# Score and value segments of an 8-head attention placed next to each other on TensorE, with the values in rotating PSUM banks and the sums of exponentials in the score banks

## The chip, the core and the metric

The kernel runs on one core of one Trainium2 chip. The metric is the device time of one execution in microseconds, here the median of three runs: 2110.87 us (2109.59 to 2112.22).

## The reference, cut

Four attention blocks follow each other on a tensor of 64 images, 256 channels and 14 by 14 pixels (196 tokens). The first (L0) has a depthwise convolution, keys and values resized to 7 by 7, and a small network behind it. The second (L1) is a linear attention. The third (L2), which the change touches, is a full attention with 8 heads of 32 channels. The fourth (L3) is a full attention with one head.

```python
hid = _group_norm(xr, norm_w, norm_b)
qkv = jnp.einsum('oc,bcl->bol', qkv_w, hid) + qkv_b[None, :, None]
...
weight = jnp.einsum('bhct,bhcs->bhts', q * scale, k * scale)
weight = jax.nn.softmax(weight.astype(jnp.float32), axis=-1).astype(weight.dtype)
a = jnp.einsum('bhts,bhcs->bhct', weight, v)
...
h = jnp.einsum('oc,bcl->bol', proj_w, h) + proj_b[None, :, None]
...
return (x + h) / RESCALE
```

## The kernel before

**Pairs and turns.** Two images make a pair, and 32 pairs run through a software pipeline. A turn of the loop starts one pair and ends one; in between some seven pairs are at work, each at another stage. What an engine does in a turn, and in which order, stands in five dictionaries (`SP_AT`, `PE_AT`, `ACT_AT`, `DVE_AT`, `POOL_AT`): each step has a number, its remainder by 128 is its place in the turn and its quotient is the number of turns by which its pair lags. The numbers are places and no times: an engine runs its list in order and waits, by semaphores, for what a step needs. The function `step` of each engine goes over the 128 places.

**Names of the steps.** L0: `q0`, `k0`, `v0`, `s0` (scores), `t0` (transposes), `o0`, `pw`, `mlp`. L1: `kv0` to `kv3`, `keys` (keys scaled by ScalarE), `q1`, `ctx0` and `ctx1` (keys by values), `out`. L2: `hq`, `hk`, `hv` (queries, keys, values), `sc0` to `sc3`, `tn`, `av0` to `av3`, `proj`. L3: `q3`, `v3`, `s3`, `t3`, `o3`. Ahead of L1, L2 and L3 stands a group norm: `gn1` to `gn3` on TensorE is a product of 8 columns with a matrix of ones by group.

**L2 in detail.** The 16 head-images of a pair are worked on in four groups g of four heads (HG = 4).
- `sc{g}` (from L1240 on): TensorE takes the four heads side by side, each in 32 rows of the array, once for each half of the tokens: eight products of 98 by 196, each head into a PSUM bank of its own (`ps_s`, four banks). In f32 each product is two instructions, so the trace shows 16.
- `max{g}_{m}` (L958): VectorE takes the maxima of two banks.
- `sc{g}_{j}` of ScalarE (L822): two exponentials for each head, with their sums through the accumulator output into `den2` in SBUF. Each is followed by an accumulator read in the trace.
- `rden{g}_{m}` (L1063): VectorE's reciprocals of four sums (two heads by two halves).
- `less{g}_{j}` (L830): ScalarE scales the exponentials.
- `tn{g}_{j}` (L1222): TensorE transposes them back into the same bank; ScalarE copies them to `pt2` (L836).
- `av{g}` (L1226): TensorE multiplies by the values, four heads side by side, each in 32 columns of the array: again 16 instructions, into bank 0 of `ps_s`. ScalarE and VectorE read the result as a high and a low part (L843, L1069).

A matmul that uses only 32 rows or only 32 columns of the array is called tiled below, one that uses it whole is called whole.

**Banks.** PSUM has eight banks. Four are `ps_s`. The other four, `a`, `b`, `c`, `e`, are plain: the steps listed for each in `BANK_USES` use it one after the other in the order of TensorE's list. A step may fill a bank when all readers of the step before it in that bank have read. The helper `product` and most matmuls go through `mm` (L1167), so the tile, not the line, tells the step.

The score banks' uses before are:

```python
bank_s = [Bank(f"bank_s{j}", ps_s[:, j], [
    use for g in range(GROUPS) for use in (
        (f"sc{g}_{j}", PE_AT[f"sc{g}"], 2), (f"tn{g}_{j}", PE_AT[f"tn{g}_{j}"], 1),
        *([(f"av{g}", PE_AT[f"av{g}"], 1)] if j == 0 else []))]) for j in range(HG)]
```

**TensorE's order in a turn, before** (places 0 to 127): tn2_1, gn2, tn2_2, k0, tn2_3, tn2_0, o3_0, pw1, **sc3**, s0_0, q3_1, v3_1, **av2**, v3_2, s0_1, mlp0, mlp1, q3_0, v3_0, v3_3, tn3_1, tn3_0, tn3_2, hk0, tn3_3, hq0, gn1, v0, t0_0, t0_1, **sc0**, s3_0, o0_1, o0_0, hv1, **av3**, hv0, s3_1, tn0_1, hq1, tn0_0, tn0_2, proj1, tn0_3, hk1, proj0, **sc1**, kv0, kv1, **av0**, kv2, t3_0, kv3, gn3, q1_0, tn1_1, q1_1, q0_1, tn1_3, tn1_0, tn1_2, ctx0, ctx1, **sc2**, q0_0, t3_1, out0, out1, **av1**, o3_1, pw0.

## Time and profile before

| | |
|---|---|
| median of three runs | 2110.87 us |
| the profiled execution | 2112.12 us |
| its span | 2109.7 us |
| granted TensorE clock, mean over the span | 0.98 |
| chain that ended last, share of the span | TensorE 88%, ScalarE 4%, VectorE 1% |
| HBM read and written | 30.85 and 12.85 MB |

The profiled execution took 2112.12 us, of which the span from its first to its last instruction is 2109.7 us. In the rows PE is TensorE's matmuls, PEld its weight loads, DVE VectorE, ACT ScalarE, POOL GpSimd, SP the engine that issues the DMAs. Busy time is the union of an engine's instructions. Matmuls overlap in the records, since they are pipelined, so the time that a block of them takes is best read from its start to the start of the next block. A row of the timeline merges instructions of the same line and tile; a bracket at its end gives the idle time of its engine before it and what ended that.

### The profile page before, as it was taken

The page shows a single profiled execution, that of the slowest core. Times are in us where ns is not written, and L with a number is a line of the kernel's source. Part 1 is how long each engine was busy: PE and PEld are TensorE (multiplying, and loading weights), DVE is VectorE, ACT ScalarE, POOL GpSimd, SP SyncE. Part 2 cuts the span into 40 slices and gives each one's busy share as a digit, 9 for nine tenths or more (in the row PEclk, how much of TensorE's full clock was granted, in tenths as well). Part 3 has the DMA queues.
Part 4 walks back from the last instruction along what each step waited for, and adds up shares of the span by engine and source line. Part 5 has one row for each costly group of instructions (what it writes and reads, how often), then busy time and mean ns, then how long its engine had stood idle before and what let it go on. Part 6 is the DMA issues. An engine that isn't in the chain of part 4 may idle for free.

```text
span 2109.7 us, 57712 instructions
## 1 busy us (share of the span) xinstructions
PE 2011.4 (95%) x15232; PEld 1689.6 (80%) x15232; DVE 1843.0 (87%) x4683; ACT 1886.4 (89%) x6231; POOL 973.3 (46%) x1707
## 2 busy tenths in 40 slices
PE   4589999999999999999999999999999999999977
PEld 3367888888888888888888888888888888888766
DVE  6789999999999999999999999999999999997532
ACT  2269999999999999999999999999999999999984
POOL 3544544545444454544445454444545544453211
PEclk8799999999999999999999999999999999999988
DMA  4000011001101100110111011011101101000000
GB/s 129 16 24 24 17 40 40 24 30 38 38 23 38 38 30 24 38 38 23 38 38 36 18 38 38 23 38 38 38 15 38 38 27 34 31 32 17 24 24 39
DMA packets 29819, 70.31 MB, mean 33 GB/s; under 512 B 6252, under 2 KB 7088, under 8 KB 29744
## 3 DMA queue, kind: packets, MB, share of 16 engines
q1 hardware_dynamic: 26928, 67.68, 9.1%
q10 hardware_dynamic: 2816, 1.72, 0.3%
q8 instruction: 36, 0.59, 0.1%
q14 instruction: 39, 0.32, 0.0%
HBM read 30.85 MB, written 12.85 MB: 21 GB/s over the span
## 4 chain that ended last, share of the span: by engine, by line
PE 88%; ACT 4%; DVE 1%; issue 1%; DVEq 0%; ACTq 0%
PE ps_e L1167 21%; PE ps_c L1167 21%; PE ps_b L1167 15%; PE ps_a L1167 11%; PE ps_s L1167 10%; PE ps_s L1222 8%; ACT e L830 1%; PE ps_a L1469 1%; ACT e L822 1%; ACT pt L836 0%; PE ps_e L1298 0%; PE ps_a L1298 0%; DVE nm L958 0%; ACT e L877 0%; ACT kv L742 0%
## 5 line engine op out<-in xcount | busy, mean ns | idle before, releaser
L822 ACT ACTIVATE e<-ps_s,nm 98x196 f32<-98x196 f32 x1024 | 423.9, 436 | 36.2 <-DVE nm L958 32.0
L830 ACT ACTIVATE e<-e,rden 98x196 f32<-98x196 f32 x1024 | 403.2, 462 | 0.2 <-DVE rden L1063 0.2
L1159 DVE SCALAR_TENSOR_TENSOR y<-opad,w_dw,y 128x406 f32<-128x406 f32 x512 | 314.9, 666 | 0.0
L1140 DVE SCALAR_TENSOR_TENSOR y<-xpad,w_dw,y 128x406 f32<-128x406 f32 x512 | 298.4, 636 | 0.0
L587 POOL TENSOR_SCALAR xn<-x,gn_scale,gn_shift 128x196 f32<-128x196 f32 x384 | 286.1, 757 | 20.8 <-POOL gn_shift L582 20.8
L575 POOL TENSOR_TENSOR gn_t<-gn_group 128x4 f32<-128x4 f32 x96 | 27.7, 289 | 563.7 <-DVE gn_group L1008 430.1
L958 DVE TENSOR_REDUCE nm<-ps_s 98x4 f32<-98x784 f32 x256 | 239.4, 966 | 34.2 <-PE ps_s L1167 34.2
L836 ACT COPY pt<-ps_s 98x392 f32<-98x392 f32 x512 | 233.3, 502 | 4.7 <-PE ps_s L1222 2.8
L1222 PE MATMUL ps_s<-w_eye,e 98*98 98x98 f32 x2048 | 228.9, 249 | 7.3 <-ACT e L830 7.2
L1222 PEld LDWEIGHTS ps_s<-w_eye,e 98*98 98x98 f32 x2048 | 200.5, 130 | 38.8 <-issue 22.3
L822 ACT ACTIVATION_READ_ACCUMULATOR e<-ps_s,nm 98x1 f32 x1024 | 222.7, 217 | 0.0
L599 POOL TENSOR_TENSOR p<-s,r 98x392 f32<-98x392 f32 x64 | 64.3, 1005 | 225.5 <-DVE r L981 225.5
L1167 PE MATMUL ps_c<-xs,ws_q 128*128 128x392 f32 x768 | 166.8, 352 | 0.0
L1167 PEld LDWEIGHTS ps_c<-xs,ws_q 128*128 128x128 f32 x768 | 133.0, 189 | 0.1
L1093 DVE TENSOR_TENSOR xs<-xn,xs 128x392 fp32r<-128x392 f32 x192 | 115.6, 603 | 16.8 <-ACT xs L781 15.4
L581 POOL TENSOR_TENSOR gn_t<-gn_group,gn_scale 128x4 f32<-128x4 f32 x96 | 123.3, 1285 | 7.5
L1167 PE MATMUL ps_s<-k,q 32*98 32x196 f32 x2048 | 118.6, 345 | 8.3 <-ACT q L791 2.3
L1167 PE MATMUL ps_s<-pt,v 98*32 98x196 f32 x2048 | 112.5, 337 | 6.8 <-ACT e L822 6.3
L1167 PEld LDWEIGHTS ps_s<-k,q 32*98 32x98 f32 x2048 | 77.4, 160 | 49.3 <-issue 28.0
L1167 PE MATMUL ps_a<-ws_v,xs 128*98 128x256 f32 (+1 forms) x768 | 112.3, 288 | 0.9 <-ACT opad L721 0.7
L1167 PEld LDWEIGHTS ps_a<-ws_v,xs 128*98 128x98 f32 x768 | 94.6, 163 | 21.6 <-issue 10.3
L939 DVE BATCH_NORM_STATS2 gn_stats<-x 128x6 f32<-128x196 f32 x384 | 109.7, 347 | 1.1
(223 smaller groups left out, 5326.6 us busy)
## 6 DMA issues: line engine op xcount, KB each, us to landing
x_in<-in_x SPq DMA_DIRECT2D x32, 392.0 KB, 3.2
x_res<-in_x SPq DMA_DIRECT2D x32, 392.0 KB, 3.1
x2b<-x SPq DMA_DIRECT2D x32, 392.0 KB, 2.7
out<-x SPq DMA_DIRECT2D x32, 392.0 KB, 2.6
out_pairs<-out SPq DMA_DIRECT2D x32, 392.0 KB, 2.5
...
```

What stands on the lines that cost most here:

```text
L581: link(g.tensor_tensor(t.t[:], t.group[:, 0], t.scale[:], ALU.mult))
L587: g.tensor_scalar(dst[:, c, of_image(i)], src[:, c, of_image(i)], t.scale[:, j:j + 1], t.shift[:, j:j + 1], ALU.mult, ALU.add).then_inc(t. ...
L822: s.activation(e2[:, j, tc], tile(use)[0:HALF, of_image(tc)], ACT.Exp, bias=nm2[:, j, tc:tc + 1], accum_out=den2[:, 2 * i + tc, h:h + 1]). ...
L830: s.activation(e2[:, j, tc], e2[:, j, tc], ACT.Copy, scale=rden2[:, 2 * i + tc, h:h + 1]).then_inc(p2_done[j].sem, 1)
L836: s.copy(turned(j), tile(use)[0:HALF, 0:N2]).then_inc(emptied(use), 1)
L939: v.bn_stats(t.stats[:, j], src[:, j // 2, of_image(j % 2)]).then_inc(t.stat_steps.sem, 1)
L958: v.tensor_reduce(out=nm2[:, two], in_=ps_s[0:HALF, two, 0:N2].rearrange("p b (c n) -> p b c n", c=2), axis=AX.X, op=ALU.max, negate=True) ...
L1093: v.tensor_tensor(dst[:, 1, c], src[:, c], dst[:, 0, c], ALU.subtract).then_inc(gn[n].low.sem, 1)
L1140: v.scalar_tensor_tensor(out=dst, in0=window(xpad, c, k, CR), scalar=tap, in1=dst, op0=ALU.mult, op1=ALU.add).then_inc(conv1_steps.sem, 1)
L1159: v.scalar_tensor_tensor(out=dst, in0=window(opad, c, k, CR), scalar=tap, in1=dst, op0=ALU.mult, op1=ALU.add).then_inc(conv2_steps.sem, 1)
L1167: return nc.tensor.matmul(dst, lhsT, rhs, start=start, stop=stop)
L1222: last = nc.tensor.transpose(tile(use)[0:HALF, of_tile(sc, tc)], e2[:, j, tc, sc * HALF:(sc + 1) * HALF], eye[0:HALF, 0:HALF])
```

## The change

The values (`av`) no longer go into bank 0 of the score banks but into the plain banks, where they rotate with the other steps. The sums of exponentials no longer go into `den2` in SBUF but into two columns of each head's score bank, 392 and 393, which the scores (392 columns) leave free; the reciprocals read them from there, with their output's axes in the matching order. `den2` is dropped. All orders but SP's are written anew (GpSimd's steps keep their order), and the plain banks are handed out anew.

In the new order of TensorE the tiled steps stand in five places of the turn: gn2, **sc3, av2**; gn1, **sc0, av3**; **sc1, av0**; gn3, **sc2**; **av1**. The whole turn is: tn2_3, tn2_1, tn2_2, o3_0, pw1, gn2, **sc3**, **av2**, s0_0, q3_1, s0_1, v3_0, mlp0, mlp1, v3_2, q3_0, tn3_1, tn3_0, v3_1, hk0, t0_0, tn3_3, tn3_2, hq0, v0, v3_3, gn1, **sc0**, **av3**, t0_1, s3_0, o0_0, hv0, o0_1, hk1, hv1, tn0_1, tn0_0, tn0_2, s3_1, hq1, proj1, tn0_3, proj0, **sc1**, **av0**, kv0, kv1, t3_0, kv3, kv2, q1_0, tn1_0, tn1_3, tn1_2, tn1_1, q1_1, q0_1, gn3, **sc2**, ctx0, ctx1, q0_0, t3_1, **av1**, out1, out0, o3_1, pw0, k0, tn2_0. On VectorE proj0 comes ahead of max1_0 and max1_1 before, and behind them now.

```diff
--- before.py
+++ after.py
@@ -41,58 +41,57 @@
 }
 
 PE_AT = {
-    "q0_1": 102, "q0_0": 115, "k0": 133, "s0_0": 144, "s0_1": 153, "v0": 176, "t0_0": 178, "t0_1": 180, "o0_1": 185,
-    "o0_0": 187, "pw0": 254, "pw1": 268, "mlp0": 283, "mlp1": 284, "gn1": 302, "kv0": 340, "kv1": 342, "kv2": 346,
-    "kv3": 349, "q1_0": 353, "q1_1": 356, "ctx0": 365, "ctx1": 367, "out0": 374, "out1": 376, "gn2": 385, "hk0": 425,
-    "hq0": 429, "sc0": 438, "hv1": 445, "hv0": 448, "tn0_1": 452, "hq1": 454, "tn0_0": 456, "tn0_2": 457,
-    "tn0_3": 461, "hk1": 463, "sc1": 466, "av0": 472, "tn1_1": 483, "tn1_3": 488, "tn1_0": 490, "tn1_2": 492,
-    "sc2": 497, "av1": 506, "tn2_1": 512, "tn2_2": 515, "tn2_3": 519, "tn2_0": 521, "sc3": 526, "av2": 533,
-    "tn3_1": 548, "tn3_0": 549, "tn3_2": 551, "tn3_3": 555, "av3": 575, "proj1": 587, "proj0": 593, "gn3": 607,
-    "q3_1": 658, "v3_1": 659, "v3_2": 663, "q3_0": 670, "v3_0": 672, "v3_3": 674, "s3_0": 695, "s3_1": 706,
-    "t3_0": 731, "t3_1": 757, "o3_1": 764, "o3_0": 778,
+    "q0_1": 106, "q0_0": 113, "k0": 121, "s0_0": 145, "s0_1": 147, "t0_0": 166, "v0": 172, "t0_1": 184, "o0_0": 189,
+    "o0_1": 195, "pw0": 248, "pw1": 268, "mlp0": 283, "mlp1": 285, "gn1": 309, "kv0": 341, "kv1": 342, "kv3": 344,
+    "kv2": 345, "q1_0": 350, "q1_1": 361, "ctx0": 367, "ctx1": 368, "out1": 372, "out0": 374, "gn2": 397, "hk0": 421,
+    "hq0": 426, "sc0": 438, "hv0": 447, "hk1": 453, "hv1": 454, "tn0_1": 455, "tn0_0": 458, "tn0_2": 460, "hq1": 462,
+    "tn0_3": 464, "sc1": 467, "av0": 468, "tn1_0": 484, "tn1_3": 486, "tn1_2": 487, "tn1_1": 488, "sc2": 492,
+    "av1": 499, "tn2_0": 508, "tn2_3": 519, "tn2_1": 521, "tn2_2": 522, "sc3": 526, "av2": 527, "tn3_1": 546,
+    "tn3_0": 547, "tn3_3": 551, "tn3_2": 553, "av3": 567, "proj1": 591, "proj0": 594, "gn3": 619, "q3_1": 658,
+    "v3_0": 660, "v3_2": 670, "q3_0": 673, "v3_1": 676, "v3_3": 691, "s3_0": 697, "s3_1": 717, "t3_0": 727,
+    "t3_1": 754, "o3_1": 759, "o3_0": 779,
 }
 
 ACT_AT = {
-    "bn0": 9, "bn1": 12, "q0_1": 121, "q0_0": 130, "k0": 147, "exp0_0": 158, "exp0_1": 166, "t0_0": 184, "v0": 185,
-    "t0_1": 187, "o0_0": 190, "o0_1": 193, "relu0": 276, "act0_high0": 278, "relu1": 279, "act0_high1": 280,
-    "high1_0": 336, "high1_1": 340, "kv0": 350, "kv1": 358, "kv2": 359, "keys0": 360, "keys1": 361, "kv3": 363,
-    "keys2": 365, "keys3": 368, "q1_0": 369, "q1_1": 370, "ctx0": 375, "ctx1": 379, "high2_0": 424, "high2_1": 427,
-    "hk0": 435, "hq0": 439, "sc0_0": 444, "sc0_1": 445, "sc0_2": 448, "sc0_3": 450, "less0_1": 454, "less0_0": 455,
-    "hv1": 456, "less0_2": 457, "tn0_1": 459, "less0_3": 460, "hq1": 461, "tn0_0": 462, "tn0_3": 465, "tn0_2": 466,
-    "hk1": 467, "hv0": 470, "sc1_0": 473, "sc1_1": 475, "sc1_2": 476, "sc1_3": 477, "less1_0": 481, "less1_1": 482,
-    "av0": 483, "less1_3": 484, "less1_2": 492, "tn1_3": 494, "tn1_1": 499, "tn1_2": 500, "tn1_0": 502, "sc2_1": 508,
-    "sc2_0": 509, "sc2_3": 512, "sc2_2": 513, "av1": 515, "less2_1": 516, "less2_2": 518, "less2_3": 519,
-    "less2_0": 523, "tn2_1": 525, "tn2_2": 526, "tn2_0": 528, "tn2_3": 530, "sc3_0": 537, "sc3_1": 540, "av2": 541,
-    "less3_0": 545, "sc3_3": 547, "sc3_2": 548, "less3_1": 551, "less3_2": 553, "less3_3": 557, "tn3_2": 560,
-    "tn3_0": 562, "tn3_3": 564, "tn3_1": 566, "av3": 579, "high3_0": 648, "high3_1": 657, "q3_1": 667, "v3_1": 672,
-    "v3_2": 674, "q3_0": 684, "v3_0": 686, "v3_3": 689, "s3_0": 708, "probs3_0": 727, "s3_1": 728, "t3_0": 736,
-    "probs3_1": 760, "t3_1": 766,
+    "bn0": -43, "bn1": 3, "q0_1": 121, "q0_0": 127, "k0": 149, "exp0_0": 162, "exp0_1": 170, "t0_0": 180, "v0": 186,
+    "t0_1": 190, "o0_0": 193, "o0_1": 196, "relu0": 274, "act0_high0": 279, "relu1": 280, "act0_high1": 281,
+    "high1_0": 331, "high1_1": 332, "kv0": 348, "kv1": 355, "kv2": 367, "keys0": 369, "keys1": 370, "q1_0": 371,
+    "kv3": 373, "q1_1": 374, "keys2": 375, "keys3": 376, "ctx0": 380, "ctx1": 381, "high2_0": 421, "high2_1": 423,
+    "hk0": 432, "hq0": 441, "sc0_1": 445, "sc0_0": 447, "sc0_2": 448, "sc0_3": 450, "less0_1": 451, "less0_0": 453,
+    "less0_2": 454, "hv0": 455, "hk1": 457, "hv1": 461, "less0_3": 462, "tn0_2": 463, "hq1": 464, "tn0_0": 465,
+    "tn0_1": 466, "tn0_3": 467, "sc1_1": 471, "av0": 472, "sc1_3": 473, "sc1_0": 474, "sc1_2": 475, "less1_0": 477,
+    "less1_1": 478, "less1_2": 479, "less1_3": 480, "tn1_0": 485, "tn1_3": 489, "tn1_2": 490, "tn1_1": 496,
+    "sc2_1": 507, "sc2_0": 510, "sc2_3": 513, "av1": 514, "less2_0": 517, "sc2_2": 518, "less2_1": 519,
+    "less2_3": 520, "less2_2": 521, "tn2_0": 522, "tn2_3": 525, "tn2_2": 528, "tn2_1": 529, "sc3_0": 539,
+    "sc3_1": 540, "av2": 543, "sc3_3": 544, "sc3_2": 545, "less3_0": 547, "less3_1": 550, "less3_3": 552,
+    "less3_2": 556, "tn3_0": 558, "tn3_1": 561, "tn3_2": 566, "tn3_3": 567, "av3": 572, "high3_0": 644,
+    "high3_1": 655, "q3_1": 669, "v3_0": 676, "v3_2": 681, "q3_0": 683, "v3_1": 687, "v3_3": 699, "s3_0": 714,
+    "s3_1": 724, "probs3_0": 726, "t3_0": 740, "probs3_1": 762, "t3_1": 768,
 }
 
 DVE_AT = {
...
-    "rden0_0": 443, "rden0_1": 448, "max1_0": 463, "max1_1": 465, "rden1_0": 469, "rden1_1": 472, "av0": 483,
...
+    "rden0_0": 434, "rden0_1": 444, "max1_0": 463, "max1_1": 464, "av0": 466, "rden1_0": 469, "rden1_1": 471,
...
 }
 
 POOL_AT = {
-    "resize0": 96, "resize1": 112, "probs0": 160, "probs1": 176, "gn1": 336, "gn2": 400, "gn3": 640, "rows3": 704,
+    "resize0": 96, "resize1": 112, "probs0": 175, "probs1": 181, "gn1": 336, "gn2": 400, "gn3": 640, "rows3": 704,
 }
 
 BANK_USES = {
-    "a": ("t0_1", "o0_1", "gn1", "ctx0", "hv0", "gn3", "v3_2", "v3_0", "t3_0", "t3_1", "o3_1",),
-    "b": ("k0", "v0", "o0_0", "mlp0", "q1_0", "ctx1", "out1", "v3_1", "v3_3", "s3_1",),
-    "c": ("q0_0", "s0_0", "pw0", "kv1", "kv3", "q1_1", "hq0", "hq1", "hk1", "q3_0", "s3_0", "o3_0",),
-    "e": ("q0_1", "s0_1", "t0_0", "pw1", "mlp1", "kv0", "kv2", "out0", "gn2", "hk0", "hv1", "proj1",
-          "proj0", "q3_1",),
+    "a": ("s0_0", "t0_0", "o0_0", "gn1", "q1_0", "ctx0", "out1", "hk1", "av0", "proj1", "v3_0", "q3_0", "o3_0",),
+    "b": ("q0_1", "k0", "t0_1", "mlp0", "kv0", "out0", "hk0", "hv0", "q3_1", "v3_3", "s3_1", "t3_0", "t3_1",),
+    "c": ("v0", "mlp1", "kv1", "kv2", "q1_1", "ctx1", "gn2", "hq1", "av1", "av2", "v3_1", "s3_0", "o3_1",),
+    "e": ("q0_0", "s0_1", "o0_1", "pw0", "pw1", "kv3", "hq0", "hv1", "av3", "proj0", "gn3", "v3_2",),
 }
 LAST_LAG = max(max(at.values()) for at in (SP_AT, PE_AT, ACT_AT, DVE_AT, POOL_AT)) // SLOTS
 
@@ -238,7 +237,6 @@
         v2 = sb("v2", [HALF, 2, 2, CH])
         nm2 = sb("nm2", [HALF, HG, 2])
         e2 = sb("e2", [HALF, HG, 2, TOK])
-        den2 = sb("den2", [HALF, 4, H2])
         pt2 = sb("pt2", [HALF, HG, 2, TOK])
         as2 = sb("as2", [128, 2, 2, KC, TOK], F32R)
         rden2 = sb("rden2", [HALF, 4, H2])
@@ -290,8 +288,7 @@
                  for b in "abce"}
         bank_s = [Bank(f"bank_s{j}", ps_s[:, j], [
             use for g in range(GROUPS) for use in (
-                (f"sc{g}_{j}", PE_AT[f"sc{g}"], 2), (f"tn{g}_{j}", PE_AT[f"tn{g}_{j}"], 1),
-                *([(f"av{g}", PE_AT[f"av{g}"], 1)] if j == 0 else []))]) for j in range(HG)]
+                (f"sc{g}_{j}", PE_AT[f"sc{g}"], 2), (f"tn{g}_{j}", PE_AT[f"tn{g}_{j}"], 1))]) for j in range(HG)]
         home = {use: bank for bank in (*banks.values(), *bank_s) for use in bank.lag}
 
         def tile(use):
@@ -816,11 +813,10 @@
                             p = pair_of(t, u, ACT_AT[use])
                             if p is not None:
 
-                                h = HG * (g % 2) + j
                                 act.wait_ge(max2_done.sem, max2_done.at(p, 2 * g + j // 2 + 1))
                                 for tc in range(2):
                                     s.activation(e2[:, j, tc], tile(use)[0:HALF, of_image(tc)], ACT.Exp,
-                                                 bias=nm2[:, j, tc:tc + 1], accum_out=den2[:, 2 * i + tc, h:h + 1]
+                                                 bias=nm2[:, j, tc:tc + 1], accum_out=tile(use)[0:HALF, N2 + tc:N2 + tc + 1]
                                                  ).then_inc(emptied(use), 1)
                             p = pair_of(t, u, ACT_AT[f"less{g}_{j}"])
                             if p is not None:
@@ -1060,8 +1056,8 @@
                                 for j in (2 * m, 2 * m + 1):
                                     dve.wait_ge(*read(p, f"sc{g}_{j}"))
                                 h = HG * (g % 2) + 2 * m
-                                v.reciprocal(rden2[:, 2 * i:2 * i + 2, h:h + 2], den2[:, 2 * i:2 * i + 2, h:h + 2]
-                                             ).then_inc(rden_done.sem, 1)
+                                v.reciprocal(rden2[:, 2 * i:2 * i + 2, h:h + 2].rearrange("p t h -> p h t"),
+                                             ps_s[0:HALF, 2 * m:2 * m + 2, N2:N2 + 2]).then_inc(rden_done.sem, 1)
                         use = f"av{g}"
                         p = pair_of(t, u, DVE_AT[use])
                         if p is not None:
```

## Rows read from the trace of the kernel before

**Rows 1.** page section 1 (busy us, share of the span, instructions by engine)

```profile
PE 2011.4 (95%) x15232; PEld 1689.6 (80%) x15232; DVE 1843.0 (87%) x4683; ACT 1886.4 (89%) x6231; POOL 973.3 (46%) x1707
```

**Rows 2.** windows view of one turn (stretch, us, busy by engine with counts, PEclk, DMA, GB/s)

```profile
1000.00:1061.34 61.34, 61.22 (x476) 51.83 (x475) 57.19 (x146) 58.60 (x195) 30.34 (x54) 1.00 0.09 33
```

**Rows 3.** timeline of TensorE around sc3 and av2 (start us, us, line, tile, form, count)

```profile
1029.88 1.52 PE L1167 MATMUL ps_c<-qt,v3t 98*128 98x196 f32 x8
1031.24 1.48 PE L1167 MATMUL ps_e<-y,w_o 128*128 128x392 f32 x4
1032.65 0.92 PE L1167 MATMUL ps_s<-k,q 32*98 32x196 f32 x16
1033.50 0.93 PE L1167 MATMUL ps_c<-k,q 128*98 128x98 f32 x8
1034.21 1.31 PE L1167 MATMUL ps_e<-xs,ws_q 128*128 128x392 f32 x6
1035.37 0.89 PE L1167 MATMUL ps_b<-ws_v,xs 128*98 128x258 f32 x6
1036.18 0.88 PE L1167 MATMUL ps_s<-pt,v 98*32 98x196 f32 x16
1036.99 0.95 PE L1167 MATMUL ps_a<-ws_v,xs 128*98 128x258 f32 x6
1037.78 0.85 PE L1167 MATMUL ps_e<-k,q 128*98 128x98 f32 x8
1038.41 1.33 PE L1167 MATMUL ps_b<-xs,ws_mlp 128*128 128x392 f32 x6
...
1040.66 1.23 PE L1167 MATMUL ps_c<-xs,ws_q 128*128 128x392 f32 x6
1041.73 0.89 PE L1167 MATMUL ps_a<-ws_v,xs 128*98 128x258 f32 x6
1042.45 0.87 PE L1167 MATMUL ps_b<-ws_v,xs 128*98 128x258 f32 x6
```

**Rows 4.** timeline of TensorE around gn3

```profile
1009.66 0.28 PE L1167 MATMUL ps_a<-gn_mine,w_group 128*128 128x8 f32 x2
1009.80 1.32 PE L1167 MATMUL ps_b<-xs,ws_q 128*128 128x392 f32 x6
1010.96 0.50 PE L1222 MATMUL ps_s<-w_eye,e 98*98 98x98 f32 x4
```

**Rows 5.** timeline of TensorE at sc1, and at ctx0, ctx1 and sc2

```profile
1001.83 0.92 PE L1167 MATMUL ps_s<-k,q 32*98 32x196 f32 x16
...
1014.75 1.92 PE L1167 MATMUL ps_a<-kv 98*128 98x256 f32 x8
1016.50 1.89 PE L1167 MATMUL ps_b<-kv 98*128 98x256 f32 x8
...
1018.51 0.92 PE L1167 MATMUL ps_s<-k,q 32*98 32x196 f32 x16
```

**Rows 6.** timeline of ScalarE from the exponentials of sc1 to the copies tn1

```profile
1004.09 0.42 ACT L822 ACTIVATE e<-ps_s,nm 98x196 f32<-98x196 f32 x1 [0.23 <-DVE nm L958]
1004.41 0.19 ACT L822 ACTIVATION_READ_ACCUMULATOR e<-ps_s,nm 98x1 f32 x1
1004.50 0.41 ACT L822 ACTIVATE e<-ps_s,nm 98x196 f32<-98x196 f32 x1
...
1008.47 0.49 ACT L884 COPY qt<-ps_a 98x392 f32<-98x392 f32 x1 [0.54 <-PE ps_a L1469]
...
1014.92 0.51 ACT L742 ACTIVATE kv<-kv,rk 98x256 f32<-98x256 f32 x1
...
1016.93 1.24 ACT L836 COPY pt<-ps_s 98x392 f32<-98x392 f32 x3
```

**Rows 7.** page section 5 and lines view (205 to 1880 us): accumulator reads; reciprocals

```profile
L822 ACT ACTIVATION_READ_ACCUMULATOR e<-ps_s,nm 98x1 f32 x1024 | 222.7, 217 | 0.0
...
L1063 DVE RECIPROCAL rden<-den 98x4 f32<-98x4 f32 x218 | 36.9, 169 | 0.1
```

20 rows, old and new, of the table DVE_AT are left out of this document.

## The prediction

> **What bounds the kernel now.** I read the page first: TensorE is busy for 95% of the span, more than any other engine [rows 1]. Then one turn of the loop (one pair of images enters and one leaves) by its stretch of the windows view: of 61.34 us TensorE is busy 61.22 at a granted clock of 1.00, ScalarE 58.60, VectorE 57.19, GpSimd 30.34 [rows 2]. So TensorE sets the turn, and ScalarE stands only 2.7 us behind it. That the matmul row is full doesn't say that columns stream all the time; for that I read the timeline, block by block, from start to start.
>
> A plain f32 matmul of 196 columns takes (1031.24 - 1029.88) / 8 = 0.17 us [rows 3]. A score group sc or a value group av holds four rounds of four matmuls side by side, so 0.68 us would do. What it takes, with what it does to its neighbours [rows 3]:
> - sc3: 33.50 - 32.65 = 0.85, so 0.17 too much inside; the block behind it (s0_0) takes 34.21 - 33.50 = 0.71, where its twin s0_1 takes 38.41 - 37.78 = 0.63, 0.08 too much.
> - av2: 36.99 - 36.18 = 0.81, 0.13 too much inside; the block ahead of it takes 36.18 - 35.37 = 0.81 and the one behind 0.79, where the two v3 blocks with no tiled neighbour take 0.72 and about as much (41.73 to 42.45): 0.09 and 0.07 too much.
> So each crossing between the whole array and its quarters is a hole of 0.15 to 0.2 us in which nothing streams. A turn has eight segments, so sixteen such holes.
>
> **The change part by part, per turn.**
> 1. *Merged segments.* By the new order of the TensorE list sc3 and av2, sc0 and av3, sc1 and av0 stand next to each other; sc2 and av1 stay alone. Of each merged pair, the 0.08 that sc cost the block behind it and the 0.09 that av cost the block ahead of it are gone: 0.17. I leave the holes inside both (0.17 and 0.13), which takes it that going from quarters by rows (sc: 32 rows) to quarters by columns (av: 32 columns) is a crossing too. No row shows such a crossing; the lower bound of the gain is 0 (it costs as much as two), the upper is all but one entry and one exit, 0.30. Three pairs by 0.17: **0.5 us** (0 to 0.9).
> The Trainium skill, TensorEngine Tiling (Array Packing), Key Properties, says that a change of the tiling mode, not of the tile alone, drains TensorE; the trace agrees for whole to tiled and back (the 0.17 and 0.13 above), and by that rule the 0.5 stands, without it 0.9.
> 2. *The small group-norm matmuls.* gn3 takes 9.80 - 9.66 = 0.14 for 8 columns, and the q1 block behind it 10.96 - 9.80 = 1.16, where a block of the same shape behind its like takes 41.73 - 40.66 = 1.07 [rows 3, 4]: 0.23 in all, a hole again, by my reading because 8 columns are too short to hide the load of the next weights. In the new order gn2, gn1 and gn3 each stand directly ahead of a tiled segment (sc3, sc0, sc2), where a hole comes anyway. I take 0.15 of each 0.23 as shared: **0.45 us** (0 to 0.7).
> 3. *A wait.* Now ctx1 and sc2 follow each other; ctx1 takes 18.51 - 16.50 = 2.01 before sc2 starts, where ctx0 takes 1.75 [rows 5]; 0.09 of the 0.26 is the crossing, 0.17 a wait of sc2. It moves away with sc2: **0.15 us** (0 to 0.17).
> Sum: 1.1 us less TensorE time, a turn of 60.2 if nobody else is late.
> 4. *What is late next: ScalarE before ctx1.* From the start of sc1 (1001.83) ScalarE has to run exponentials, keys and copies until the last key is scaled, 1014.92 + 0.51 = 1015.43, that is 13.6 us later; ctx1, which needs it, starts at 1016.50 [rows 5, 6]: 1.1 us to spare. In the new ScalarE order three more copies tn1 stand ahead of that last key (1.24 for three), and so do the four exponentials of q1, which now come behind it (1016.93 - 1014.92 less 0.41 for the key: 1.6) [rows 6]; on the other side the wait of 0.54 before the copy of t3_0 has no place any more, since that copy now comes later. So 13.6 + 1.2 + 1.6 - 0.5 = 15.9 us. TensorE's work from sc1 to ctx1 is 1016.50 - 1001.83 = 14.7 now, gains sc2 (0.85 and 0.1 around it) and loses the 0.17 and 0.15 of above: 15.3. ctx1 would wait 0.6; the first exponential may start some tenths sooner than the 2.26 us behind sc1 of now (VectorE now adds up the proj blocks ahead of its maxima there, and in the new order one of them only behind), so I take a give-back of **0.45 us** (0 to 1.1). Behind the waiting ctx1 on TensorE stand q0_0, t3_1, av1 and the out blocks, all of which slide.
> 5. *Sums of exponentials in the score banks.* 32 accumulator reads per turn now write one column of PSUM. The read costs 0.217 mean [rows 7], but the next exponential starts 0.09 behind its start (1004.41, 1004.50) [rows 6], so I take it at nothing; no ScalarE instruction of this trace writes PSUM, so its price is bounded by the row that writes SBUF: at best the 0.09 goes, -2.9 us of ScalarE per turn, at worst all of the read is exposed, 0.13 by 32, +4.1. The nearest row is the same read into another memory, hence zero.
> 6. *The reciprocal reads PSUM.* Eight of 0.169 per turn [rows 7]; were they twice as long, 1.4 us more on VectorE, which has 4.1 idle [rows 2]: nothing, as long as that idle time covers it; without it, at most 1.4.
> 7. *Values in plain banks, no den2.* The same instructions into other banks: no time of their own. It takes av out of score bank 0, so that the next sc need not wait for av's two readers, which is what lets an av follow an sc at all. No DMA is added or moved past others; SP's list is unchanged, GpSimd's keeps its order.
>
> Net: 1.1 - 0.45 = 0.68 us per turn (unrounded 1.13). Of 32 pairs I count 30 turns, since the first and the last pairs run in turns that are only partly filled: 20 us. The profiled execution took 2112.1 us (span 2109.7 and 2.4 around it), 1.3 above the median of 2110.9 of the runs shown. 2112.1 - 20.4 - 1.3 gives **2090 us**.
>
> **Rivals.** About 0.2%, 4 us, is what a measurement of this kernel can tell from no change.
> - *ScalarE keeps up*: ctx1 doesn't wait. For it: ScalarE's exponentials queue behind waits of theirs now, and those can shrink. Against it: the count above. 1.13 by 30 is 34 us: 2077.
> - *Quarters to quarters without a crossing*: the pair runs on, the upper bound of part 1: 0.13 more of each pair, 0.4 per turn. For it: nothing in the trace, which has no such pair; against it: every change between whole and tiled costs. With the give-back 1.08 by 30 is 32 us, 2078; without it 1.5 by 30, 2066. It would go against the rule of the Trainium skill named in part 1.
> - *ScalarE takes all of it back*: at a turn of 60.2 its 58.6 busy leave 1.6 idle, and it has 2.7 of waits now [rows 2]. If the waits of ScalarE and of TensorE don't shrink, the holes that close become waits at ctx1, at sc0 (behind the copy of hq0) and at the transposes. Nothing measurable: 2107 to 2115.
> - *Slower: the accumulator read into PSUM is exposed*. Its place is the 32 reads; it decides from (61.34 - 58.60) / 32 = 0.085 us each, where ScalarE fills the old turn. At 0.12 each, 3.8 us, ScalarE is busy 62.4; with 0.9 of waits that stay, 63.3 per turn, 2.0 by 30 more: 2171. For it: these exponentials are the largest group of ScalarE. Against it: the read is pipelined now with its write to SBUF.
> The Trainium skill, ScalarE: Activation LUTs, has ScalarE nearer to PSUM than to SBUF, which speaks against this rival; no run here shows it.
> That the change doesn't do what it says (an av that waits for its transposed copies right behind its sc, so that the hole is a wait) falls under the third.
>
> **Numbers.** Forecast with a give-back of 0.2 to 1.0 per turn (2082 to 2106) 0.40; ScalarE keeps up 0.27; no crossing inside a pair 0.08; all taken back 0.14; slower 0.11. So faster 0.75, same 0.14, slower 0.11. The range goes from 2064 (just below the second rival's 2066) to 2113 (most of the third rival); outside are the slower rival and a few per cent below. The likeliest case's own range is 2082 to 2106.
>
> **What would show it.** In the changed kernel's timeline: sc3 to the start of the block behind av2 should take 0.85 + 0.81 or less; the blocks behind gn should no longer be long; a turn should be near 60.7. The waits of TensorE's weight loads at ctx1 should be about 0.4 by turn and name ScalarE's keys. The accumulator read should still be followed 0.09 us later by the next exponential. I am wrong if the turn stays at 61.3 (waits in place of holes), or ScalarE's exponentials stretch, or a pair's inner crossing costs as much as two.

## The result and the profile after

The changed kernel takes 2169.24 us, median of 4 runs (2167.92 to 2174.7), against 2111.05 for the kernel before (4 runs, 2109.59 to 2112.22): a ratio of 1.028 with a 95% interval of 1.0265 to 1.0296. 2090 was forecast; it is 58 us slower, not 21 faster. Its profiled execution took 2169.64 us, the span 2167.9. Lines of the code stand three or four higher than before (L1167 is L1163, L822 is L818, L781 is L778).

The page's section 1:

```profile
PE 2007.3 (93%) x15232; PEld 1702.0 (79%) x15232; DVE 1856.4 (86%) x4683; ACT 1855.9 (86%) x6231; POOL 1062.2 (49%) x1707
```

The windows view of one turn (columns as in [rows 2]):

```profile
1000.00:1063.10 63.10, 60.93 (x476) 51.95 (x475) 57.58 (x146) 57.55 (x195) 33.44 (x53) 1.00 0.09 32
```

Against [rows 1, 2]: TensorE is busy 4 us less in all and 0.29 less in a turn, ScalarE 1.05 less in a turn, and the turn has become 63.1 us long (sc3 starts at 1000.72 and again at 1063.85) where it was 61.34. 30 turns by 1.76 are 53 of the 58 us. TensorE's and ScalarE's work got cheaper; what was added is waiting. The waits views, ScalarE's and TensorE's over the whole span (us in total, times, longest):

```profile
ACT xs L778 <- POOL xn L584: 84.4, 66, 5.3
...
PE ps_s L1218 <- ACT e L826: 52.1, 33, 4.1
PE ps_s L1163 <- ACT pt L832: 14.0, 22, 1.7
```

The same three in the kernel before:

```profile
ACT xs L781 <- POOL xn L587: 3.0, 3, 1.8
...
PE ps_s L1222 <- ACT e L830: 7.2, 12, 1.2
PE ps_s L1167 <- ACT pt L836: 2.4, 5, 1.0
```

L778 is `high1`: ScalarE's high part of the normalised images that enter L1. How it comes to hold up TensorE is read in three timelines of the same stretch. TensorE:

```profile
1015.88 0.28 PE L1163 MATMUL ps_a<-gn_mine,w_group 128*128 128x8 f32 x2
1016.09 0.92 PE L1163 MATMUL ps_s<-k,q 32*98 32x196 f32 x16
...
1028.42 1.24 PE L1163 MATMUL ps_a<-as,ws_p 128*128 128x392 f32 x6
1031.14 0.51 PE L1218 MATMUL ps_s<-w_eye,e 98*98 98x98 f32 x4 [1.49 <-ACT e L826]
1031.43 1.32 PE L1163 MATMUL ps_e<-as,ws_p 128*128 128x392 f32 x6
1033.33 0.92 PE L1163 MATMUL ps_s<-k,q 32*98 32x196 f32 x16 [0.58 <-ACT pt L832]
```

ScalarE:

```profile
1027.36 0.52 ACT L778 CAST xs<-xn 128x392 fp32r<-128x392 f32 x1 [0.89 <-POOL xn L584]
1029.28 0.52 ACT L778 CAST xs<-xn 128x392 fp32r<-128x392 f32 x1 [1.40 <-POOL xn L584]
1029.71 0.58 ACT L807 COPY v<-ps_e 98x512 f32<-98x512 f32 x1
1030.19 0.81 ACT L826 ACTIVATE e<-e,rden 98x196 f32<-98x196 f32 x2
```

GpSimd:

```profile
1017.24 0.30 POOL L609 TENSOR_SCALAR rb<-v3t,bqk 98x4 f32<-98x4 f32 x1 [4.19 <-ACT v3t L848]
...
1018.09 0.20 POOL L572 TENSOR_TENSOR gn_t<-gn_group 128x4 f32<-128x4 f32 x1
1018.37 2.89 POOL L573 TENSOR_TENSOR gn_v<-gn_group,gn_t 128x4 f32<-128x4 f32 x1
...
1024.45 4.80 POOL L584 TENSOR_SCALAR xn<-x,gn_scale,gn_shift 128x196 f32<-128x196 f32 x4 [0.22 <-POOL gn_shift L579]
```

GpSimd ends `xn` at 1029.25. The two copies `high1` stand ahead of `hv1`, `less0_3` and the copies `tn0` in ScalarE's new list, wait 0.89 and 1.40 for it, and everything behind them is 2.3 us late. tn0_3 on TensorE, due behind proj1, needs `less0_3` and waits 1.49; sc1 needs the bank that the copy of tn0_3 empties and waits 0.58 more. Together these are 2.1 us of the turn, more than the 1.8 by which it grew.

The same places in the kernel before (TensorE's gn1 and sc0, ScalarE's first `high1`, GpSimd's gn1 from its first to its last operation):

```profile
1046.74 0.28 PE L1167 MATMUL ps_a<-gn_mine,w_group 128*128 128x8 f32 x2
...
1048.59 0.92 PE L1167 MATMUL ps_s<-k,q 32*98 32x196 f32 x16
...
1060.48 0.53 ACT L781 CAST xs<-xn 128x392 fp32r<-128x392 f32 x1
...
1047.39 0.47 POOL L575 TENSOR_TENSOR gn_t<-gn_group 128x4 f32<-128x4 f32 x1 [0.81 <-DVE gn_group L1008]
...
1054.24 3.84 POOL L587 TENSOR_SCALAR xn<-x,gn_scale,gn_shift 128x196 f32<-128x196 f32 x4 [0.22 <-POOL gn_shift L582]
```

Counted from sc0: `xn` was ready at 1058.08, 9.5 us behind it, and is now 13.2 behind it. Of the 3.7, 1.64 is that gn1 moved from 1.85 ahead of sc0 to 0.21 ahead; 1.56 that GpSimd starts it 2.21 behind TensorE's gn1 and not 0.65 (its list has `rows3` first, which needs the copy of v3_3, and v3_3 moved to directly ahead of gn1); 0.47 that it takes longer. ScalarE meanwhile comes to `high1` earlier: it is free for it at 1026.47 (1027.36 less the wait), 10.4 us behind sc0, where `high1_0` began 11.9 behind it before. There were 2.4 us to spare; now 2.8 are missing until the whole of `xn` is ready.

The holes did close. The timeline of TensorE around sc3 and av2, and of ScalarE at the exponentials of sc3:

```profile
999.19 1.48 PE L1163 MATMUL ps_e<-y,w_o 128*128 128x392 f32 x4
1000.51 0.28 PE L1163 MATMUL ps_c<-gn_mine,w_group 128*128 128x8 f32 x2
1000.72 0.92 PE L1163 MATMUL ps_s<-k,q 32*98 32x196 f32 x16
1001.57 0.87 PE L1163 MATMUL ps_c<-pt,v 98*32 98x196 f32 x16
1002.37 0.93 PE L1163 MATMUL ps_a<-k,q 128*98 128x98 f32 x8
...
1002.78 0.42 ACT L818 ACTIVATE e<-ps_s,nm 98x196 f32<-98x196 f32 x1 [0.20 <-DVE nm L954]
1003.10 0.16 ACT L818 ACTIVATION_READ_ACCUMULATOR e<-ps_s,nm 98x1 f32 x1
1003.15 0.43 ACT L818 ACTIVATE e<-ps_s,nm 98x196 f32<-98x196 f32 x1
```

From sc3 to the block behind av2 it is 0.85 + 0.80, as part 1 had it. gn takes 0.21 ahead of a tiled block; before it took 0.14 and cost 0.09 behind it, and sc3 cost the block ahead of it 0.09 (1.41 in [rows 3], 1.32 now): about 0.1 saved each, not 0.15. And the next exponential starts 0.05 behind the accumulator read, where it was 0.09 [rows 6].

### The profile page after: what moved, and what is told of

The parts are those of the page before. It is cut to its first block and busy times, and to the rows that moved or that the text cites. A ratio compares the mean times of both kernels' runs of the same rounds, so it can differ in the third digit from the quotient of the medians.

```text
span 2167.9 us, 57840 instructions
## 1 busy us (share of the span) xinstructions
PE 2007.3 (93%) x15232; PEld 1702.0 (79%) x15232; DVE 1856.4 (86%) x4683; ACT 1855.9 (86%) x6231; POOL 1062.2 (49%) x1707
## 5 line engine op out<-in xcount | busy, mean ns | idle before, releaser
L818 ACT ACTIVATE e<-ps_s,nm 98x196 f32<-98x196 f32 x1024 | 424.8, 493 | 36.6 <-DVE nm L954 36.5
L584 POOL TENSOR_SCALAR xn<-x,gn_scale,gn_shift 128x196 f32<-128x196 f32 x384 | 321.7, 850 | 20.5 <-POOL gn_shift L579 20.5
L1218 PE MATMUL ps_s<-w_eye,e 98*98 98x98 f32 x2048 | 208.9, 250 | 52.4 <-ACT e L826 52.1
L818 ACT ACTIVATION_READ_ACCUMULATOR e<-ps_s,nm 98x1 f32 x1024 | 247.8, 245 | 0.0
L778 ACT CAST xs<-xn 128x392 fp32r<-128x392 f32 x192 | 105.8, 554 | 86.2 <-POOL xn L584 84.4
L1089 DVE TENSOR_TENSOR xs<-xn,xs 128x392 fp32r<-128x392 f32 x192 | 133.8, 710 | 49.9 <-ACT xs L778 49.7
L1163 PE MATMUL ps_s<-k,q 32*98 32x196 f32 x2048 | 121.4, 352 | 19.4 <-ACT pt L832 14.0
L576 POOL TENSOR_TENSOR gn_y<-gn_v,minus_half 128x4 f32<-128x4 f32 x96 | 112.6, 1173 | 8.0
L579 POOL TENSOR_TENSOR gn_shift<-w_gn_b,gn_t 128x4 f32<-128x4 f32 x96 | 105.9, 1103 | 7.5
L1163 PEld LDWEIGHTS ps_s<-k,q 32*98 32x98 f32 x2048 | 78.7, 163 | 32.5 <-issue 24.9
L1163 PE MATMUL ps_e<-y,w_o 128*128 128x392 f32 x256 | 97.9, 505 | 5.0 <-DVE y L1155 5.0
L1163 PE MATMUL ps_c<-ws_kv,xs 128*98 128x512 f32 x384 | 100.7, 398 | 0.0
L1163 PE MATMUL ps_b<-ws_v,xs 128*98 128x256 f32 (+1 forms) x576 | 88.5, 298 | 1.7 <-ACT pt L711 1.7
```

Source lines behind the costliest of these rows:

```text
L576: link(g.tensor_tensor(t.y[:], t.v[:], minus_half[:], ALU.pow))
L584: g.tensor_scalar(dst[:, c, of_image(i)], src[:, c, of_image(i)], t.scale[:, j:j + 1], t.shift[:, j:j + 1], ALU.mult, ALU.add).then_inc(t. ...
L818: s.activation(e2[:, j, tc], tile(use)[0:HALF, of_image(tc)], ACT.Exp, bias=nm2[:, j, tc:tc + 1], accum_out=tile(use)[0:HALF, N2 + tc:N2 + ...
L1089: v.tensor_tensor(dst[:, 1, c], src[:, c], dst[:, 0, c], ALU.subtract).then_inc(gn[n].low.sem, 1)
L1163: return nc.tensor.matmul(dst, lhsT, rhs, start=start, stop=stop)
L1218: last = nc.tensor.transpose(tile(use)[0:HALF, of_tile(sc, tc)], e2[:, j, tc, sc * HALF:(sc + 1) * HALF], eye[0:HALF, 0:HALF])
```

## The experiments

The theory after the result: ScalarE's list, `high1` waiting for GpSimd, is the whole loss. Rivals: the sums in PSUM cost it, or merging itself does. The numbers in the lists are places; only the entries that differ are shown.

**1. The copies high1 back behind hq1**, in the changed kernel (ScalarE's list, and VectorE's low parts with it; `less0_3` and `tn0_2` come ahead).

```diff
 ACT_AT
-    "high1_0": 331, "high1_1": 332, "hv1": 461, "less0_3": 462, "tn0_2": 463, "hq1": 464, "tn0_0": 465, "tn0_1": 466,
+    "hv1": 459, "less0_3": 460, "tn0_2": 461, "hq1": 462, "high1_0": 335, "tn0_0": 464, "tn0_1": 465, "high1_1": 338,
 DVE_AT
-    "low1_0": 328, "low1_1": 329, "conv2_0": 202, "s3_1": 715, "proj1": 588, "r3_0": 717,
+    "conv2_0": 200, "s3_1": 713, "low1_0": 330, "proj1": 587, "r3_0": 716, "low1_1": 333,
```

> The changed kernel with one thing moved: ScalarE's two casts high1 (which wait for GpSimd's group norm gn1) stand behind less0_3 and the first copies tn0 instead of ahead of them, and VectorE's low1 one to three places later with them; nothing is left out. Theory (ScalarE's queue is held up by high1, which waits 2.3 us a turn for GpSimd, and less0_3, tn0_3 and sc1 stand behind it): the 1.7 us ahead of tn0_3 and most of the 0.7 us ahead of sc1 go, a turn falls from 63.1 to about 61.0 us, the time to 2095 to 2115. Rival (ScalarE's sums in PSUM or the merged segments themselves cost the time): unchanged, 2160 to 2175.

Measured: 2110.81 us (10 runs), ratio to the kernel before 0.9999 (0.9989 to 1.0008). All 58 us are back: the place of these few steps is the loss. But the gain of 20 isn't there either. Its turn is 61.2 (sc1 at 1002.04 and 1063.25), with these rows in the timeline (TensorE, then ScalarE):

```profile
1063.25 0.92 PE L1163 MATMUL ps_s<-k,q 32*98 32x196 f32 x16 [0.44 <-ACT pt L832]
...
1060.35 0.59 ACT L788 ACTIVATE q<-ps_c,qb2s 128x392 f32<-128x392 f32 x1 [0.59 <-PE ps_c L1163]
1060.84 0.51 ACT L778 CAST xs<-xn 128x392 fp32r<-128x392 f32 x1
```

`high1` no longer waits; sc1 still does, behind an idle 0.59 of ScalarE.

**2. The kernel before with the sums of exponentials in PSUM** (both heads' sums of a pair in its odd bank), and **3. the changed kernel with the sums back in SBUF** (the reciprocals read them there again).

```diff
-  accum_out=den2[:, 2 * i + tc, h:h + 1]
+  accum_out=ps_s[0:HALF, j | 1, N2 + 2 * (j % 2) + tc:N2 + 2 * (j % 2) + tc + 1]
...
-  v.reciprocal(rden2[:, 2 * i:2 * i + 2, h:h + 2], den2[:, 2 * i:2 * i + 2, h:h + 2]
+  v.reciprocal(rden2[:, 2 * i:2 * i + 2, h:h + 2].rearrange("p t h -> p h t"),
+               ps_s[0:HALF, 2 * m + 1, N2:N2 + 4].rearrange("p (h t) -> p h t", t=2)
```
```diff
-  accum_out=tile(use)[0:HALF, N2 + tc:N2 + tc + 1]
+  accum_out=den2[:, 2 * i + tc, HG * (g % 2) + j:HG * (g % 2) + j + 1]
```

> The kernel before with the sums of exponentials alone in PSUM (both heads' sums of a pair of banks in the odd one of the two, since av still uses bank 0). Theory (a read of the accumulator into PSUM is cheaper than into SBUF): exponentials follow each other at 0.36 us instead of 0.40, ScalarE is busy 1.2 us less a turn, and the time stays within 0.3% of before, since TensorE sets the turn: 2105 to 2113. Rival (that write is what makes the changed kernel slow): 2130 or more.

> The changed kernel with the sums of exponentials back in SBUF. Theory (the cheaper read gives ScalarE 1.2 us a turn, of which part shortens the chain that TensorE waits for): slower than the changed kernel by up to 1.2 us a turn, 2170 to 2205. Rival (the sums in PSUM are what costs): 2110 to 2150.

Measured: 2109.49 us (10 runs), ratio 0.9991 (0.9981 to 1.0), and 2172.78 (4 runs), ratio 1.0294 (1.0277 to 1.0311), both to the kernel before. One turn of the second run by the windows view:

```profile
1000.00:1061.30 61.30, 61.18 (x475) 51.78 (x476) 57.15 (x146) 57.97 (x195) 30.34 (x53) 1.00 0.10 33
```

One turn of the third:

```profile
1000.00:1063.10 63.10, 60.89 (x476) 51.88 (x475) 57.52 (x146) 58.18 (x194) 33.90 (x53) 1.00 0.09 32
```

ScalarE's busy time in a turn goes down by 0.63 with the sums in PSUM [rows 2] and up by 0.63 with them in SBUF, half of the 1.2 that was expected. Either way the time moves by 1 to 4 us. The sums are no cost, and hardly a gain while ScalarE isn't the bound.

**4. The two waits of the first run taken away**: tn0_0 and tn0_1, transposed already while ScalarE idles, copied ahead of hq1, and av3 read by VectorE ahead of a depthwise step.

```diff
 ACT_AT
-    "hq1": 462, "high1_0": 335, "tn0_0": 464, "tn0_1": 465, "high1_1": 338, "tn0_3": 467,
+    "tn0_0": 462, "tn0_1": 463, "hq1": 464, "high1_0": 337, "tn0_3": 466, "high1_1": 339,
 DVE_AT
-    "conv1_3": 49, "rden0_0": 434, "av3": 563,
+    "av3": 561, "conv1_3": 50, "rden0_0": 435,
```

> The first experiment (after with the copies high1 back behind hq1) runs turns of 61.22 us, in which TensorE still waits about 0.9: 0.5 at sc1 for the copy of tn0_3, behind an idle 0.59 us of ScalarE that waits for hq1 while tn0_0 and tn0_1 are already transposed, and 0.2 at o0_1 for VectorE's read of av3, which stands behind four depthwise products. Here tn0_0 and tn0_1 are copied ahead of hq1 and av3 is read before the third of these products. Theory (the holes have been closed, what is left are waits of order): both waits go, turn 60.4 to 60.7, 2085 to 2100 us, faster than both kernels. Rival (ScalarE at 57.5 busy takes the gain back elsewhere): turn 61.1 to 61.3, 2105 to 2115.

Measured: 2116.71 us (7 runs), ratio 1.0029 (1.0018 to 1.004). That is above both ranges, with a turn of 61.6. The two waits went, and this one came, at t3_0:

```profile
1073.37 0.54 PE L1465 MATMUL ps_b<-w_eye,e 98*98 98x98 f32 x4 [1.01 <-DVE kv L1014]
```

Not ScalarE but VectorE is late there: it reads kv0 out of the bank only behind its maxima of sc1, which start 2.3 us behind sc1 in this run and 1.27 in the first.

**5. That kernel with the merged pairs taken apart** (av2 behind v3_0, av3 behind o0_0, av0 behind kv1, their readers later).

```diff
 PE_AT
-    "av2": 527, "s0_0": 145, "q3_1": 658, "s0_1": 147, "v3_0": 660, "av3": 567, "t0_1": 184, "s3_0": 697, "o0_0": 189,
+    "s0_0": 143, "q3_1": 657, "s0_1": 146, "v3_0": 659, "av2": 532, "t0_1": 183, "s3_0": 696, "o0_0": 185, "av3": 573,
...
```

> The kernel of the run before with the three merged pairs taken apart again (av2 behind v3_0, av3 behind o0_0, av0 behind kv1, their readers on ScalarE and VectorE a few steps later to match). Theory (a crossing inside a pair costs 0.135 us against 0.187 and 0.119 apart, 0.17 more for each of three pairs): TensorE busy per turn and the turn itself go up by 0.5, 10 to 18 us more than the run before. Rival (the merging was worth nothing, apart or together the same holes): within 4 us of the run before.

Measured: 2222.92 us (5 runs), ratio 1.053 (1.0513 to 1.0547). It doesn't tell what merging is worth: blocks that use the banks of av2 and av3 next now wait for VectorE's late reads, 0.66 and 0.98 in a turn, and kv2 waits another 0.96 for VectorE's read of a bank.

**6. The reverse of the first: the kernel before with high1 early**, and nothing else.

```diff
 ACT_AT
-    "less0_1": 454, "less0_0": 455, "hv1": 456, "less0_2": 457, "high1_0": 336, "high1_1": 340,
+    "high1_0": 326, "high1_1": 327, "less0_1": 456, "less0_0": 457, "hv1": 459, "less0_2": 460,
...
```

> The kernel before with one thing changed: on ScalarE the two copies high1 stand ahead of less0_1, where they start at about 1056.0 in its trace, 2.1 us before GpSimd ends gn1 (1058.1). Nothing else moves. Theory (a copy that waits for GpSimd holds everything behind it in ScalarE's queue): ScalarE waits about 2 us per turn naming xn of GpSimd, sc1 or the transposes tn0 slide, turn 62.0 to 63.3, 2130 to 2175 us. Rival (the place of these copies does not matter, ScalarE has 2.7 us idle per turn to absorb it): 2105 to 2116.

Measured: 2219.72 us (4 runs), ratio 1.0513 (1.0497 to 1.0529): in the theory's direction, and worse than its range, 3.6 us per turn. The timeline of ScalarE and TensorE:

```profile
1052.25 0.52 ACT L781 CAST xs<-xn 128x392 fp32r<-128x392 f32 x1 [0.31 <-POOL xn L587]
1054.02 0.52 ACT L781 CAST xs<-xn 128x392 fp32r<-128x392 f32 x1 [1.25 <-POOL xn L587]
...
1055.30 0.55 PE L1222 MATMUL ps_s<-w_eye,e 98*98 98x98 f32 x4 [1.92 <-ACT e L830]
...
1057.57 1.32 PE L1167 MATMUL ps_e<-as,ws_p 128*128 128x392 f32 x6
...
1118.93 0.54 PE L1222 MATMUL ps_s<-w_eye,e 98*98 98x98 f32 x4 [1.92 <-ACT e L830]
...
1121.76 2.17 PE L1167 MATMUL ps_e<-as,ws_p 128*128 128x392 f32 x6
```

Three stretches by the windows view (the clock is third from the end of a row):

```profile
1056.00:1060.00 4.00, 4.00 (x30) 3.74 (x29) 1.48 (x4) 3.78 (x10) 3.15 (x7) 1.00 0.00 0
1116.00:1120.00 4.00, 2.08 (x15) 1.75 (x14) 3.65 (x11) 2.75 (x8) 1.86 (x3) 1.00 0.00 0
1120.00:1124.00 4.00, 4.00 (x21) 3.83 (x20) 0.21 (x1) 2.67 (x8) 3.07 (x8) 0.57 0.00 0
```

The wait is the theory's (1.6 of ScalarE, 1.92 of TensorE). What made the loss larger: in many turns, not in this one but in the next, the granted clock falls from 1.00 to 0.57 for the 4 us behind the same wait, mostly the lower of its two levels (1.2 GHz), and the six matmuls of proj1 take 2.0 us (1121.76 to 1123.77) instead of 1.16 (1057.57 to 1058.73). From this wait to the next it is 63.6 us (1055.30 to 1118.93), and from there, with the fall, 65.3 (to 1184.19): about 2.3 us over the old turn without it, and 1.6 more with it. So the 109 us are not the wait alone.

**7. A depthwise step ahead of VectorE's copy for gn1 and the maxima of sc0**, in the fourth kernel.

```diff
 DVE_AT
-    "gn1": 301, "max0_0": 430, "max0_1": 431, "conv1_2": 48,
+    "conv1_2": 45, "gn1": 302, "max0_0": 431, "max0_1": 432,
```

> The fourth experiment ended 0.5 us per turn where 0.7 was to be won: its trace has the waits at sc1 and o0_1 gone and a new one of 1.0 at t3_0 in their place, which waits for VectorE to read kv0 out of the bank. VectorE has no idle time from its maxima of sc0 (1053.98) to that read (1072.57), 2.3 us behind sc1 it only begins the maxima of sc1. Ahead of the maxima of sc0 it idles 0.82 and 0.78. Here one depthwise step (conv1_2, two products, 1.1 us) goes from behind these maxima to ahead of gn1, into that idle time. Theory (VectorE's queue between sc0 and t3_0 is the last wait in the turn): the wait at t3_0 goes, turn 60.4 to 60.8, 2082 to 2100 us, faster than both kernels. Rival (some other queue is next): turn 61.1 or more, 2105 us or more.

Measured: 2105.42 us (10 runs), ratio 0.9975 (0.9965 to 0.9984): faster than both kernels, by 0.25% against the kernel before, but far from the theory's range and inside the rival's. The wait at t3_0 halved:

```profile
1065.52 0.54 PE L1465 MATMUL ps_b<-w_eye,e 98*98 98x98 f32 x4 [0.56 <-DVE kv L1014]
```

**8. One block between each merged pair, and ScalarE's read of av0 three steps later**, in that kernel.

```diff
 PE_AT
-    "av2": 527, "s0_0": 145, "av3": 567, "t0_1": 184, "av0": 468, "kv0": 341,
+    "s0_0": 143, "av2": 529, "t0_1": 183, "av3": 568, "kv0": 340, "av0": 469,
 ACT_AT
-    "av3": 572, "sc0_1": 445, "av0": 472, "sc1_3": 473, "sc1_0": 474, "sc1_2": 475,
+    "sc0_1": 444, "av3": 573, "sc1_3": 472, "sc1_0": 473, "sc1_2": 474, "av0": 475,
```

> The run before with one whole block put between each merged pair (sc3, s0_0, av2; sc0, t0_1, av3; sc1, kv0, av0) and ScalarE's reads of av3 and av0 one and three steps later. Theory (crossings: a merged pair saves 0.17 us): turn 0.5 longer than the run before, 10 to 18 us more. Rival (merging saves nothing): within 4 us of it. A wait that names av's readers would make it inconclusive; the start-to-start times of the blocks then still tell what a crossing costs.

Measured: 2221.35 us (5 runs), ratio 1.0526 (1.0512 to 1.054), inconclusive on merging. VectorE's read of av0 needs ScalarE's, and kv0 stands behind it (VectorE, then TensorE):

```profile
1056.28 0.36 DVE L1065 TENSOR_TENSOR as<-ps_a,as 128x196 fp32r<-128x196 f32 x1 [2.15 <-ACT as L839]
...
1057.37 0.54 PE L1465 MATMUL ps_b<-w_eye,e 98*98 98x98 f32 x4 [2.60 <-DVE kv L1014]
```

The time is 116 us over the seventh run. TensorE's wait at t3_0 is 2.60 there instead of 0.56, from a read moved three places on one engine: the mechanism of the result once more. The granted clock is lower too, 0.958 over the span against 0.98, and how much of the 116 us is the clock's or the crossings' isn't told apart.

**9. A depthwise step behind the maxima of sc1**, in the seventh kernel, and **10. one block between each merged pair in the ninth**, with ScalarE's read of av0 left where it was.

```diff
 DVE_AT
-    "conv2_1": 206, "max1_0": 463, "max1_1": 464, "stats3": 600, "conv2_2": 217, "conv2_5": 240, "max2_1": 500,
+    "max1_0": 462, "max1_1": 463, "stats3": 599, "conv2_1": 216, "conv2_2": 228, "max2_1": 496, "conv2_5": 244,
...
```
```diff
 PE_AT
-    "av2": 527, "s0_0": 145, "av3": 567, "t0_1": 184, "av0": 468, "kv0": 341,
+    "s0_0": 143, "av2": 529, "t0_1": 183, "av3": 568, "kv0": 340, "av0": 469,
 ACT_AT
-    "av3": 572, "sc0_1": 445,
+    "sc0_1": 444, "av3": 573,
```

> The seventh experiment runs turns of 61.16 us with one wait left on TensorE, 0.56 to 0.59 at t3_0 for VectorE's read of kv0. VectorE starts the maxima of sc1 1.8 us behind sc1 because the depthwise step conv2_1 (1.35 us) stands right ahead of them. Here conv2_1 goes behind the statistics of the next group norm, and the steps conv2_2 to conv2_4 one place later each; the second maximum of sc2 comes ahead of conv2_5. Theory (only this queue is left): the wait at t3_0 goes, turn 60.5 to 60.7, 2082 to 2096 us. Rival (VectorE's later reads of kv2, q1 and sc2 become late in turn): turn 61 or more, 2100 us or more.

> The run before with one whole block put between each merged pair on TensorE (sc3, s0_0, av2; sc0, t0_1, av3; sc1, kv0, av0); the readers keep their order, but for the copy of av3 on ScalarE, one exponential step later. Theory (a merged pair saves 0.17 us): TensorE's blocks take 0.5 more per turn, 10 to 18 us more than the run before if that run has no waits left, less if a wait hides some of it. Rival (merging saves nothing): within 4 us of it.

Measured: the ninth 2121.48 us (5 runs), ratio 1.005 (1.0037 to 1.0064), the rival: t3_0 doesn't wait, but `high1` waits 1.90 for GpSimd again, and TensorE 0.32 and 0.42 elsewhere. The tenth 2140.29 us (4 runs), ratio 1.0135 (1.0119 to 1.015): 18.8 us more than the ninth, 0.6 per turn, just over the 10 to 18 us expected. TensorE's busy time of a turn rises by 0.75 (60.95 to 61.70, windows view), and waits shrink by the rest, so this is the size, not the second digit.

**11. kv0 read ahead of proj0 and av0**, in the seventh kernel, and **12. one more depthwise step ahead of the maxima of sc0** in the eleventh.

```diff
 DVE_AT
-    "proj0": 593, "av0": 466, "kv0": 339,
+    "kv0": 337, "proj0": 594, "av0": 467,
```
```diff
 DVE_AT
-    "max0_0": 431, "max0_1": 432, "av3": 561, "conv1_3": 50,
+    "conv1_3": 47, "max0_0": 432, "max0_1": 433, "av3": 562,
```

> The seventh experiment (2105.4 us, turns of 61.16) with one step moved on VectorE: it reads kv0 out of its bank (0.67) right behind the maxima of sc1, ahead of the sums of proj0 and av0 (0.54 and 0.27) instead of behind them. In the trace of the seventh run the read would then end at 1064.6 instead of 1065.4, and t3_0, which waits for it, could start with no wait at about 1064.95 instead of 1065.52; kv3, which needs the bank of proj0, follows 0.33 later and may wait 0.1 to 0.2. Theory (the last wait goes, and nothing else is late): turn 60.55 to 60.85, 2086 to 2097 us. Rival (as in the ninth run, another queue is late next): turn 61.1 or more, 2103 us or more.

> The eleventh experiment moved the wait from t3_0 to kv3 (0.31 in the trace, 0.55 with what the block behind t3_0 loses) and its turn stayed at 61.16: VectorE runs from the maxima of sc0 (1047.25) to its read of proj0 with 0.4 us idle, so the stretch of the turn from sc0 to kv3 has VectorE's length whatever stands first at its end. Here one more depthwise step (conv1_3, 1.1 us) goes from behind these maxima to ahead of them, into the 0.61 us that VectorE idles there; the maxima start 0.5 later. Theory (VectorE's run from sc0 to proj0 is what sets the turn): that run ends 0.6 sooner behind sc0, turn 60.5 to 60.8, 2086 to 2097 us. Rival (ScalarE's exponentials of sc0, 0.5 later, make tn0 and sc1 late instead): turn 61.0 or more, 2101 us or more.

Measured: the eleventh 2105.76 us (5 runs), ratio 0.9963 (0.995 to 0.9977), like the seventh; the twelfth 2116.52 (6 runs), ratio 1.003 (1.0018 to 1.0043). Both lie in their rivals' ranges. TensorE's timeline in the eleventh:

```profile
1005.12 1.63 PE L1163 MATMUL ps_e<-ws_kv,xs 128*98 128x512 f32 x6 [0.31 <-DVE x L1075]
```

VectorE's in the twelfth:

```profile
1056.77 0.19 DVE L1059 RECIPROCAL rden<-ps_s 98x4 f32<-98x4 f32 x1 [0.95 <-ACT e L818]
```

In the eleventh the wait only passed from t3_0 to kv3, and the turn stayed. In the twelfth VectorE, filled up ahead of the maxima, then waits 0.95 for exponentials that start later, and TensorE waits 0.30 at kv3 as before and 0.29 more for a copy of ScalarE. Between sc0 and kv3 VectorE and ScalarE run one behind the other with little idle time, and a step moved on one list comes back as a wait on the other.

## Why the prediction was wrong

*Part 1, merged segments, 0.5*: right. The inner crossing, rows to columns, costs about what one between whole and tiled does; 0.85 + 0.80 stands in the trace, and the tenth run puts 0.6 per turn on having a block inside each pair. Its rival (no crossing inside a pair) falls: the inside of sc3 and av2 is as long as before. The Trainium skill, TensorEngine Tiling (Array Packing), Key Properties, says that a change of the mode drains TensorE; the trace agrees, with 0.17 and 0.12 over plain streaming inside sc3 and av2.

*Part 2, gn, 0.45*: right in kind, too large; 0.1 for each of three. Why 8 columns leave a hole wasn't tested. And it had a price that I didn't put down: gn1 next to sc0 is a gn1 1.64 us later, and GpSimd's chain of 11 us hangs on it.

*Part 3, a wait of sc2, 0.15*: it is gone (gn3 starts at 1046.01, sc2 0.21 behind it, ctx0 0.85 behind that, with no wait).

*The sum of the three, 1.1*: not found in full. TensorE's busy time of a turn fell by 0.29 in the changed kernel, and by 0.65 in the seventh run, the fastest (columns as in [rows 2]):

```profile
1000.00:1061.16 61.16, 60.57 (x478) 51.90 (x474) 57.35 (x146) 57.48 (x195) 29.86 (x54) 1.00 0.10 33
```

Where the rest stayed isn't shown.

*Parts 5 and 6, sums in PSUM, nothing*: right for the time, within 4 us. The read is cheaper than I took it, 0.04 for each of 32 by the pitch of the exponentials (0.37 from 1002.78 to 1003.15, against 0.41 in [rows 6]), and half of that by ScalarE's busy time (0.63 per turn). The reciprocal takes 0.18 where it took 0.17. The slower rival, an exposed read, gave 2171, near what was measured, but its mechanism is refuted (runs 2 and 3): the right number for a wrong reason.

*Part 4, "What is late next: ScalarE before ctx1"*: this step failed. It followed ScalarE over one stretch, from sc1 to the last key, and gave back 0.45 at ctx1, which now starts at 1048.96 without a wait. The stretch that decided is the one before it, from sc0 to sc1: there the new list has `high1`, steps that wait for another engine, ahead of `less0_3` and tn0, steps that TensorE waits for: 2.29 us of waiting on ScalarE, and 1.49 and 0.58 on TensorE behind it. *Part 7* failed with it: "GpSimd's keeps its order" is true and beside the point, since what its steps wait for (gn1, v3_3) had moved. Runs 1 and 6 show the cause from both sides: the copies moved back return the 58 us, the copies moved forward in the kernel before cost 109, part of it through the clock.

The third rival, all taken back, is what remains once this is mended (2110.81), though at other places than I gave it: not ctx1 and sc0, but sc1 and t3_0 (transposes too, but of L3), behind ScalarE and VectorE between sc0 and kv3. The 20 us were never shown to be within reach; the best order found (runs 7 and 11) has 5 to 8 of them, by the ratios. Whether another order has more, and whether GpSimd's gn1 made earlier would let the changed order stand as it is, wasn't tried.
